# Routing scratch of a fused transformer block in PSUM, both choices in the rank products, and the tile table from one product with the matrix of ones

## The reference

```python
logits = h @ gate_weight.T
scores = softmax(logits)                                    # 8 experts
group_scores = scores.reshape(T, 4, 2).max(-1)
gidx = top_k(group_scores, 2)                               # the 2 best groups of 2 experts
masked = where(group chosen, scores, 0)
topk_w, topk_i = top_k(masked, 2)                           # the 2 best experts in them
routed = sum over the two of  expert(h) * weight
out = x + gb * (routed + shared(h))
```

## Time and profile before

| | us |
|---|---|
| median of 3 runs | 308.44 (307.14 to 309.18) |
| the profiled execution | 309.42 |
| its span in the profile | 307.7 |
| TensorE busy | 265.2 |
| VectorE busy | 200.4 |
| ScalarE busy | 159.7 |
| GpSimd busy | 138.4 |
| mean granted TensorE clock | 0.943 of full |

### The profile page before, as it was taken

One profiled execution on the slowest core, in us unless ns is written; L12 is line 12 of the kernel. 1 busy time (PEld: TensorE's weight loads), 2 busy tenths in 40 slices (PEclk: granted clock), 3 DMA queues, 4 the chain that ended last, 5 costly groups with the idle time before them and its releaser, 6 DMA issues.

```text
span 307.7 us, 6160 instructions
## 1 busy us (share of the span) xinstructions
PE 265.2 (86%) x1801; PEld 244.3 (79%) x1801; DVE 200.4 (65%) x582; ACT 159.7 (52%) x427; POOL 138.4 (45%) x156
## 2 busy tenths in 40 slices
PE   1799999889999999799985881999999999999900
PEld 1697698879899899688884681999999999999800
DVE  2667754359987745974899780155556556867894
ACT  1538468787566746565303332255656656556500
POOL 3120416453440388577974866000544445445440
PEclk9999999999999999989998596699999999999975
DMA  7891043532231022243100235322343456684554
GB/s 233 300 334 36 0 132 107 145 108 68 68 108 37 17 106 88 69 123 124 34 17 35 72 112 201 89 53 71 113 118 117 139 168 202 196 232 141 168 189 136
DMA packets 29319, 36.98 MB, mean 120 GB/s; under 512 B 4468, under 2 KB 23903, under 8 KB 29288
## 3 DMA queue, kind: packets, MB, share of 16 engines
q1 hardware_dynamic: 24056, 27.19, 29.5%
q0 software_dynamic: 3408, 8.46, 7.7%
q10 hardware_dynamic: 1824, 0.94, 1.0%
HBM read 24.78 MB, written 12.71 MB: 122 GB/s over the span
## 4 chain that ended last, share of the span: by engine, by line
PE 75%; DVE 10%; issue 5%; ACT 3%; POOL 2%; DMA 2%; ACTq 1%; POOLq 0%; DVEq 0%
PE bank L346 18%; PE bank L348 17%; PE bank L347 16%; PE bank L1128 4%; PE bank L1365 3%; PE bank L1343 3%; PE bank L1100 3%; PE bank L1083 2%; PE bank L1111 2%; PE bank L1120 2%; PE bank L1092 2%; POOL routed_in L697 1%; PE bank L1001 1%; DMA routed_out<-yo_all,dest 1%; DMA mh<-routed_out 1%
## 5 line engine op out<-in xcount | busy, mean ns | idle before, releaser
L1431 POOL DMA_INDIRECT routed_out<-yo_all,dest x39 | 40.1, 1028 | 65.7 <-ACT yo_all L1392 51.9
L346 PE MATMUL bank<-experts_w,h2T_lo 128*128 (+1 forms) x156 | 50.8, 325 | 0.1
L347 PE MATMUL bank<-experts_w,h2T_hi 128*128 (+1 forms) x156 | 47.2, 303 | 0.0
L348 PE MATMUL bank<-experts_w,h2T_hi 128*128 (+1 forms) x156 | 47.1, 302 | 0.0
L697 POOL DMA_INDIRECT routed_in<-h2all,slot_u x32 | 31.7, 990 | 14.1 <-issue 7.6
L346 PE MATMUL bank<-h2T_hi,wsgu_lo 128*128 128x256 f32 (+1 forms) x96 | 28.9, 301 | 7.1 <-issue 6.6
L1420 DVE SCALAR_TENSOR_TENSOR wstage<-wstage,wt,bank 128x176 f32<-128x176 f32 x39 | 15.5, 397 | 29.2 <-ACT wstage L1382 29.2
L346 PEld LDWEIGHTS bank<-experts_w,h2T_lo 128*128 128x128 f32 (+1 forms) x156 | 29.5, 189 | 0.5 <-issue 0.5
L347 PEld LDWEIGHTS bank<-experts_w,h2T_hi 128*128 128x128 f32 (+1 forms) x156 | 29.6, 190 | 0.1
L348 PEld LDWEIGHTS bank<-experts_w,h2T_hi 128*128 128x128 f32 (+1 forms) x156 | 29.3, 188 | 0.0
L347 PE MATMUL bank<-h2T_lo,wsgu_hi 128*128 128x256 f32 (+1 forms) x96 | 27.6, 288 | 0.0
(11 more groups left out here) (250 smaller groups left out, 791.1 us busy)
## 6 DMA issues: line engine op xcount, KB each, us to landing
h2all<-routed_in SPq DMA_DIRECT2D x39, 130.0 KB, 2.1
wstage<-gu_t SPq DMA_DIRECT2D x8, 352.0 KB
res<-x SPq DMA_DIRECT2D x4, 512.0 KB, 8.4
mx<-modrow SPq DMA_DIRECT2D x8, 256.0 KB
mh<-modrow SPq DMA_DIRECT2D x8, 256.0 KB, 3.1
exchange<-routed_out SPq DMA_DIRECT2D x8, 256.0 KB
wmod_s<-w_mod SPq DMA_DIRECT2D x3, 512.0 KB, 9.9
wstage<-down_t SPq DMA_DIRECT2D x8, 176.0 KB
```

The source lines that it names most:

```text
L346: pe.matmul(out_ap, l[1], r[0], start=start, stop=False)
L347: pe.matmul(out_ap, l[0], r[1], start=False, stop=False)
L348: return pe.matmul(out_ap, l[0], r[0], start=False, stop=stop)
L1431: pool.indirect_dma_start(out=routed_out, out_offset=bass.IndirectOffsetOnAxis(dest[:, t % 16:t % 16 + 1], 0), in_=yo[t % 6], in_offset=No ...
```

## The change

Three things change. The scratch of the choice (r_rank, and r_pos in L632) and r_slot move from SBUF to free columns of PSUM bank 7, as MATCH, REST and SLOT. r_both is gone: r_sel is kept in BF16, and each product that took r_both is made twice, once per choice, into the same sum. The table is one product of 78 columns whose weights are the matrix of ones; the factors ecol and rcol are multiplied into two one-hot matrices on VectorE. In the weights, one copy is left out, since the reciprocal is written straight into h2all. Context that is not needed is left out of the diff.

```diff
@@ -232,8 +232,8 @@
         kcol = sb("kcol", [P, 1])
-        ecol = sb("ecol", [P, 1], BF16)
-        rcol = sb("rcol", [P, 1], BF16)
+        ecol = sb("ecol", [P, 1])
+        rcol = sb("rcol", [P, 1])
         e_of = sb("e_of", [P, 1])
@@ -242,7 +242,7 @@
         pos = sb("pos", [P, 1])
-        onehot = sb("onehot", [P, NT], BF16)
+        onehot = sb("onehot", [P, 2, NT], BF16)
         unused_row = sb("unused_row", [1, NT])
@@ -283,14 +283,11 @@
-        r_rank = sb("r_rank", [P, NB, NE])
-        r_sel = sb("r_sel", [P, 2, NB, NE])
-        r_both = sb("r_both", [P, NB, NE], BF16)
+        r_sel = sb("r_sel", [P, 2, NB, NE], BF16)
         r_acc = sb("r_acc", [P, NPAIR - 1, NE], BF16)
...
         r_tmp = sb("r_tmp", [P, 2, NB, NE])
-        r_slot = sb("r_slot", [P, 2, NB])
         r_top = sb("r_top", [P, NB])
@@ -357,6 +354,9 @@
         TAB = HB[1][:, 4 * NB * NE:4 * NB * NE + 2 * NT].rearrange("p (i t) -> p i t", i=2)
+        SLOT = HB[1][:, 10 * NB * NE:10 * NB * NE + 2 * NB].rearrange("p (c t) -> p c t", c=2)
+        MATCH = HB[1][:, 8 * NB * NE:9 * NB * NE].rearrange("p (t e) -> p t e", e=NE)
+        REST = HB[1][:, 9 * NB * NE:10 * NB * NE].rearrange("p (t e) -> p t e", e=NE)
         NF = len(FT)
@@ -581,28 +581,31 @@
             pe.wait_ge(s_order_ready, 2)
-            pe.matmul(TAB[:, 0, :], ecol[:].to_broadcast([P, P]), onehot[:], start=True, stop=True)
-            pe.matmul(TAB[:, 1, :], rcol[:].to_broadcast([P, P]), onehot[:], start=True, stop=True).then_inc(s_tabmm_done, 1)
+            pe.matmul(TAB, ones[:], onehot[:], start=True, stop=True).then_inc(s_tabmm_done, 1)
...
             pe.wait_ge(s_both_ready, p + 1)
-            pe.matmul(RNK, before[:], r_both[:].rearrange("p t e -> p (t e)"), start=True, stop=False)
+            for c in range(2):
+                pe.matmul(RNK, before[:], r_sel[:, c].rearrange("p t e -> p (t e)"), start=(c == 0), stop=False)
             pe.matmul(RNK, ones[:], ebase[:].rearrange("p t e -> p (t e)"), start=False, stop=False)
...
             for j in range(NB - 1):
-                last = pe.matmul(RNK[:, (j + 1) * NE:].rearrange("p (t e) -> p t e", e=NE), ones[:],
-                                 r_both[:, j:j + 1, :].to_broadcast([P, NB - 1 - j, NE]), start=False, stop=(j == NB - 2))
+                for c in range(2):
+                    last = pe.matmul(RNK[:, (j + 1) * NE:].rearrange("p (t e) -> p t e", e=NE), ones[:],
+                                     r_sel[:, c, j:j + 1, :].to_broadcast([P, NB - 1 - j, NE]), start=False, stop=(j + c == NB - 1))
...
                 for j in range(TT):
-                    pe.matmul(CNT[:, 3:5, :], ones[:], r_both[:, j:j + 1, :].to_broadcast([P, 2, NE]), start=False, stop=False)
+                    for c in range(2):
+                        pe.matmul(CNT[:, 3:5, :], ones[:], r_sel[:, c, j:j + 1, :].to_broadcast([P, 2, NE]), start=False, stop=False)
                 for j in range(TT, NB):
-                    last = pe.matmul(CNT[:, 4, :], ones[:], r_both[:, j, :], start=False, stop=(j == NB - 1))
+                    for c in range(2):
+                        last = pe.matmul(CNT[:, 4, :], ones[:], r_sel[:, c, j, :], start=False, stop=(j + c == NB))
             last.then_inc(s_rank_done, 1)
@@ -629,22 +632,23 @@
             else:
-                n = done(dve.scalar_tensor_tensor(r_pos[:], r_sel[:, 0], -3.0e38, LG, ALU.mult, ALU.add))
+                n = done(dve.scalar_tensor_tensor(REST, r_sel[:, 0], -3.0e38, LG, ALU.mult, ALU.add))
                 dve.wait_ge(s_rt_b, n)
-                best, top, at = r_pos[:], r_second[:], r_at[:]
+                best, top, at = REST, r_second[:], r_at[:]
             n = done(dve.tensor_reduce(top, best, AX.X, ALU.max))
             dve.wait_ge(s_rt_b, n)
-            n = done(dve.tensor_tensor(r_rank[:], best, per_expert(top), ALU.is_equal))
+            n = done(dve.tensor_tensor(MATCH, best, per_expert(top), ALU.is_equal))
             dve.wait_ge(s_rt_b, n)
-            n = done(dve.scalar_tensor_tensor(r_rank[:], r_rank[:], -float(NE), eidx[:].unsqueeze(1).to_broadcast([P, NB, NE]),
+            n = done(dve.scalar_tensor_tensor(MATCH, MATCH, -float(NE), eidx[:].unsqueeze(1).to_broadcast([P, NB, NE]),
                                               ALU.mult, ALU.add))
             dve.wait_ge(s_rt_b, n)
-            n = done(dve.tensor_reduce(at, r_rank[:], AX.X, ALU.min))
+            n = done(dve.tensor_reduce(at, MATCH, AX.X, ALU.min))
             dve.wait_ge(s_rt_b, n)
-            n = done(dve.tensor_tensor(r_sel[:, c], r_rank[:], per_expert(at), ALU.is_equal))
-            dve.wait_ge(s_rt_b, n)
-            if c == 1:
-                dve.tensor_tensor(r_both[:], r_sel[:, 0], r_sel[:, 1], ALU.add).then_inc(s_both_ready, 1)
+            if c == 0:
+                n = done(dve.tensor_tensor(r_sel[:, 0], MATCH, per_expert(at), ALU.is_equal))
+                dve.wait_ge(s_rt_b, n)
+            else:
+                dve.tensor_tensor(r_sel[:, 1], MATCH, per_expert(at), ALU.is_equal).then_inc(s_both_ready, 1)
@@ -657,15 +661,15 @@
             dve.wait_ge(s_rt_exp, p + 1)
+            dve.wait_ge(s_both_ready, p + 1)
             dve.tensor_reduce(r_z[:], r_exp[:], AX.X, ALU.add)
...
             dve.tensor_reduce(r_e2[:], r_pos[:], AX.X, ALU.add)
-            n = done(dve.reciprocal(r_z[:], r_z[:]))
+            n = done(dve.reciprocal(h2all[:, kept(p), D], r_z[:]))
             dve.tensor_copy(h2all[:, kept(p), D + 3], token_id[:, p * NB:(p + 1) * NB])
             dve.wait_ge(s_rt_w, n)
-            dve.tensor_copy(h2all[:, kept(p), D], r_z[:])
-            dve.scalar_tensor_tensor(h2all[:, kept(p), D + 1], r_e2[:], 1.0, r_z[:], ALU.subtract, ALU.mult)
+            dve.scalar_tensor_tensor(h2all[:, kept(p), D + 1], r_e2[:], 1.0, h2all[:, kept(p), D], ALU.subtract, ALU.mult)
@@ -678,11 +682,11 @@
             dve.wait_ge(s_rt_c, n)
-            n = done(dve.tensor_reduce(r_slot[:], r_tmp[:], AX.X, ALU.add))
+            n = done(dve.tensor_reduce(SLOT, r_tmp[:], AX.X, ALU.add))
             dve.wait_ge(s_rt_c, n)
-            dve.tensor_copy(slot_u[:, :, p * NB:(p + 1) * NB], r_slot[:]).then_inc(s_slots_ready, 1)
+            dve.tensor_copy(slot_u[:, :, p * NB:(p + 1) * NB], SLOT).then_inc(s_slots_ready, 1)
             if p < NPAIR - 1:
-                counts = r_both[:].rearrange("p t e -> p e t")
+                counts = r_sel[:].rearrange("p c t e -> p e (c t)")
                 n = done(dve.tensor_reduce(r_sum[:], counts, AX.X, ALU.add))
@@ -739,7 +743,8 @@
             dve.wait_ge(s_tab, n)
-            dve.tensor_scalar(onehot[:], tidx[:], pos[:, 0:1], None, ALU.is_equal).then_inc(s_order_ready, 1)
+            dve.tensor_scalar(onehot[:, 0, :], tidx[:], pos[:, 0:1], ecol[:, 0:1], ALU.is_equal, ALU.mult)
+            dve.tensor_scalar(onehot[:, 1, :], tidx[:], pos[:, 0:1], rcol[:, 0:1], ALU.is_equal, ALU.mult).then_inc(s_order_ready, 1)
```

## The result

The changed kernel takes 303.84 us (median of 4 runs, 303.73 to 305.74), the kernel before 308.10 beside it (4 runs, 307.14 to 309.18): ratio 0.9865, 95% interval 0.9824 to 0.9905. That is 4.3 us won, where 11.4 were forecast. The time lies in the forecast's range (293.0 to 305.0) but not near its value of 297.0: it is the first rival's case (305.4), and that it lies in the range at all is luck, since the routing part won more than it was counted for.

A forecast was written before the change was run, and what follows sets the result against it. TensorE, busy for 86% of the span, was taken to bound the kernel. 309.42 - 5.6 - 2.8 - 1.7 - 1.6 + 0.3 = 298.0, or 297.0 us against the median; range 293.0 to 305.0.

The forecast's parts named there:

- the first rival: At the table: the stall has another cause, say scatters and pad rows, and stays; 305.4 us, chance 0.15.
- The table step: At the table product before group 6: repeated-column weights cause TensorE's stall; the ones matrix removes it, saving 5.6 us.
- the 2.8 behind it: Behind the table stall: 30 matmuls run at full clock instead of 0.52, saving 2.8 us more.
- The price of the stall: At the table: 8.4 us less on TensorE's side, 5.6 for the stall and 2.8 for the slow clock.
- The choice step: Routing, groups 1 and 2: PSUM scratch and no r_both save 1.7 (bounds 0, 3.6) and 1.6; added rank products cost 0.3.
- the second rival: VectorE against GpSimd: the port conflict only moves, h2all rows and weights lose the choice's gain; 300.3 us, chance 0.2.
- The third: Clock also stays up in 165.28 to 177.00, or group 1's choice pays in full; about 293 us, chance 0.12.
- the fourth: In the choice: VectorE's writes to PSUM are dear, so slower; 313 us with the stall kept, chance 0.04.

The follow-up runs named there:

- run 5: The kernel before with the table part of the change alone (one product with the matrix of ones): 309.17 us, ratio 1.0004.
- run 1: The changed kernel with the old table put back (two products with repeated-column weights), so the choice part alone: 304.53 us, ratio 0.985.
- run 9: The kernel before plus only the hold: group 3's scatters 3 to 7 wait until the down products (4) have signalled: 301.39 us, ratio 0.9752.
- run 4: The changed kernel with the table's product one step later in TensorE's order, behind the next up products: 305.66 us, ratio 0.9867.
- run 3: The changed kernel with GpSimd's eight scatters of group 3 held until the tile table is ready: 302.23 us, ratio 0.9782.
- run 2: The changed kernel with SyncE's eight pad-row transfers held until the tile table is ready: 305.52 us, ratio 0.9894.
- run 6: The changed kernel with each of group 3's eight scatters held until the one before it has landed: 308.91 us, ratio 0.9968.
- run 8: The changed kernel plus the hold: group 3's first three scatters start, the other five wait until the down products (4) have signalled: 297.70 us, ratio 0.9602.
- run 10: The kernel before with only the routing scratch (r_rank, r_pos in the choice, r_slot) moved to PSUM; r_both and the old table stay: 305.67 us, ratio 0.9887.
- run 11: The changed kernel with four scatters of group 3 started before the hold for the down products' signal, instead of three: 297.74 us, ratio 0.9667.
- run 7: The kernel before with each of group 3's eight scatters held until the one before it has landed: 312.34 us, ratio 1.0077.

## Why the prediction was wrong

**The table step failed,** 5.6 us of the 11.4, and the 2.8 behind it. It took the repeated column for the cause of the late signal, because it found no other weight load like it, and concluded that the array stood still. Runs 5 and 1 put the form of the table at nothing in both kernels, run 9 has the repeated columns without a stall, run 4 a stall without a table. What stands behind the stall is GpSimd's row of eight scatters, with the pad rows moving beside it: TensorE's completion signals are held back while the row goes on, and most are let go at its end or up to 1.9 us later (in run 3 the first of three was let go 1.2 us before it). Taking either away from this place (runs 2, 3, 6 and 8) takes the stall away. First and last scatter of the row, in the kernel before and then in the changed one:

```profile
180.66 0.99 POOL L697 DMA_INDIRECT routed_in<-h2all,slot_u  x1 [0.16 <-issue]
...
189.75 0.96 POOL L697 DMA_INDIRECT routed_in<-h2all,slot_u  x1 [0.30 <-issue]
```

```profile
174.88 0.99 POOL L701 DMA_INDIRECT routed_in<-h2all,slot_u  x1 [0.16 <-issue]
...
183.82 0.96 POOL L701 DMA_INDIRECT routed_in<-h2all,slot_u  x1 [0.31 <-issue]
```

In each kernel the row begins 4.4 us before the down product ends (185.06 and 179.29) and lasts 10 us; L477 starts at 190.69, when the row ends (190.71), and at 186.43, 1.6 us after (184.78), which is the longer stall. All of this was in the trace of before: the first rival even names the scatters and pad rows, and got 0.15. The step took a coincidence that occurs once for a cause, and its argument "it was the array that stood still" was wrong too: in run 3 three products end at 185.23, 186.64 and 188.07 while TensorE works on (with idle pieces of at most 1.0 us), and their signals come at 189.89, 192.85 and 192.98. The array was not halted; TensorE waited for L477, and L477 for TensorE's own signal.

**The price of the stall was about right:** 8.4 us were put on stall and slow clock, and the hold gives 7.1 in the kernel before (run 9), within a fifth, and in the changed one (run 8) 6.1 by the medians, 7.6 by the spans. With the stall gone the changed kernel takes 297.7 us, where the forecast said 297.0 with the table as the reason; that the two agree is no merit of that step. The slow clock went with the wait (1.00 in run 8), as its term assumed.

**The choice step was right, and undersized.** It forecast 1.7 + 1.6 - 0.3 = 3.0 us; the medians give 4.3 (the change, 2.9 to 5.4 by its interval, which still takes in 3.0) and 4.8 (run 1, whose table costs nothing), the traces 3.6 before the stall. With the hold in both kernels (runs 8 and 9) the change is worth 3.7 us, by the medians and by the spans net of the start-up alike. By place, group 1 gave 2.3 us (1.7 forecast) and group 2 another 1.2 (1.6 forecast). In group 1 the slow stretch behind the rank products is gone, a gain that the forecast had only in its upper bound, though part of the conflict moved, as the second rival said (L666's 1.23 us). In group 2 only the wait of 1.20 us on r_both is gone. The h2all rows and slot_u came sooner by that much and no more, where the step had them gain on the rank products as well: from these to the transposes it takes 9.1 us now (150.29 to 159.39), with L670's 5.37 us in them, against 9.0 before (156.30 to 165.28), and the wait on slot_u kept its size (2.21 against 2.17). The second rival's time, 300.3, needed all of the gain lost. Run 10 divides the gain: all of group 1's lead at the rank products and 2.5 of the 3.6 us before the stall come from the scratch, the rest from r_both.

**The first rival** had the right place for the cause and 305.4; the measured 303.84 is that with the larger choice. **The third** (clock, or group 1 in full) and **the fourth** (writes to PSUM dear) did not come: in 159.39 to 171.00, which answers to 165.28 to 177.00, the granted clock is 0.56 again over 8.91 us of work, group 1 gave 2.3 and not 3.6, and every step on the new scratch took 0.17 to 0.23 us in all groups. The rule of the Trainium skill that was weighed there, 120 cycles for a PSUM source against 58 for SBUF (VectorE: DVE Perf Modes, The TRN2 errata), isn't seen here either: 0.20 us for L640 with an operand and the result in the bank.

The other rule, by which a column step of 0 is inside what the fast weight load allows (the Trainium skill, TensorE: Matmul & The Clock Gate, Weight-path perf modes), agrees with run 9: 0.10 us for the repeated column, as for the matrix of ones. Another page would have warned of the reading itself: in the Trainium skill's Perfetto Trace Analysis, Tensor Engine Instruction, a matmul's end in the profile is computed, and its signal is sent only when PSUM has acknowledged the bytes. By that page the 7.1 us between L345's end and L477's start need not be the array's time; where in that path they lie no run here shows.

**What stays open.** Why a row of scatters holds TensorE's signals isn't shown, nor why not ScalarE's or VectorE's (in run 3 ScalarE's L443 ends at 185.06 in the midst of the row, and VectorE starts on it at 185.09). Nor is the number that it takes: three before the hold did nothing to down(4) in run 8, yet three behind one another are followed by the 1.9 us at the rank products. The two need not differ in kind: in run 8 down(4) ends 0.9 us after the third scatter's instruction (179.73), and in run 11 the signal came 1.0 us after the fourth's, so in run 8 it may have come too late to be held. That pads make it worse is one observation (0.6 us late in run 2 against 7.1), and signals in the midst of a row are not always late: in run 8 a product that ends at 183.01, 2.1 us into the five scatters, is heard at once.

## What to carry to other kernels

When the profile says "issue" or "remote" and the work waited for had long ended by its row, look at what every other engine and queue does in just that stretch, and move each of them once before an edit is made for one. Eight indirect scatters in a row, with other transfers beside them, can cost more than their own time: end the row ahead of the signal that TensorE waits for, and let the rest fall where TensorE has work; one at a time was dearer still. When a conflict between VectorE and GpSimd on SBUF is taken from one step, the next step that reads and writes only SBUF can have it (L666, L670 and r_both here); count that one too.

## What the runs showed of the hardware

- TensorE's signals came up to 7.1 us after the modelled end of the product (usually 14 ns) while GpSimd started scatters every 1.27 us beside the pad transfers, up to 6.2 us without these (run 3), and were let go together (down(4)'s at 186.40 and the table's at 186.44 in the changed kernel); TensorE executed on meanwhile where it had work (run 3).
- Scatters of 128 rows, each held until the one before had landed, started 2.7 to 4.2 us apart (runs 6 and 7); in a row they start every 1.27 us.
- A 128x4 copy on VectorE lasted 5.37 us while GpSimd ran four operations on SBUF, and ended with the last of them.
- The start-up's product with wvT started between 17.5 and 20.1 us in executions of kernels that do the same up to there: 2.6 us of spread to be taken off before two profiles are compared.
